# Four chained layers on one core: row statistics of three norms taken by ScalarE one stage earlier

## Chip, cores and metric

The kernel runs on one core of a Trainium2 chip, as one launch. The metric is the device time of a run in microseconds (us), lower is better; several runs are taken and their median counts. Engines are named PE (TensorE), DVE (VectorE), ACT (ScalarE), POOL (GpSimd) and SP (SyncE, which here only issues transfers).

## Reference, cut to what matters

A batch of 4 x 512 tokens with 256 channels passes through four layers, all in float32:

```python
def _layernorm(x, axis=-1, eps=1e-05):
    m = jnp.mean(x, axis=axis, keepdims=True)
    v = jnp.var(x, axis=axis, keepdims=True)
    return (x - m) / jnp.sqrt(v + eps)

x = L0_attn_x
xn = _layernorm(x); x = x + scan_attention(xn) + mlp(xn)                  # layer 0
xn = _layernorm(x); x = x + dilated_attention(xn) + moe_32_experts_top4(xn) # layer 1
xn = _layernorm(x); x = x + chunk_abc(xn) + mla_block_with_8_experts(xn)    # layer 2
xn = _layernorm(x); x = x + causal_attention(xn) + moe_8_experts_top2(xn)   # layer 3
```

The change concerns the second, third and fourth of these layer norms. The bodies of the layers are shortened to names here.

## The kernel before

The 2048 tokens are 16 tiles of 128 rows. `core.x` holds x in SBUF as [128, 16, 256]; `core.xn` holds the normalised rows, in rows of 260 columns whose last four, `core.marks`, are free until a routing writes its marks into them. The program is a sequence of blocks. In a block each engine has its own instruction stream, and at its end all five engines meet, so the next block starts when the last engine is done. The blocks that matter:

- `layer0_join` (j0): PE multiplies, ACT copies, POOL and DVE add, DVE takes statistics of another norm; then DVE alone writes `core.x` tile by tile (L807 the gain, L803 the sum, signalled by `added`).
- `slots_route` for layer 1 (p1) with `Normalise` n1: DVE takes the statistics (`part_stats`, L258 to L275) of tiles 0 to 7 and 8 to 15, POOL raises the variance to the power -0.5 (L304), DVE writes the normalised rows (L288), PE turns each tile (L319), ACT copies it into `xnT` (L338), and the routing follows: PE's logits, DVE's top choices and row numbers, then 64 indirect transfers by POOL (L2487), beside which the dilated attention runs.
- `slots_experts` (f1), the 32 experts. It ends with `add_pairs` (L2855), 64 additions of DVE into `core.x`, 8 for each group of two tiles.
- `NormaliseSplit` (n2): the same norm, but ACT copies each turned tile rounded (L403), DVE takes the rest (L389), and at the eighth tile ACT waits for the first six weight transfers and rounds the weights (L401).
- `layer2_abc`, `layer2_attention`, then `experts` (f2), eight dense experts in 32 steps of 512 tokens. `weigh` (L2421) adds each step's four tiles into `core.x` and raises `y_taken`. PE is saturated there until the last steps.
- `slots_route` for layer 3 (p3): PE first multiplies two weights (L3326, 16 matmuls), which ACT copies (L3332, L3335), ACT loads a table (L350), and then comes `Normalise` n3 as above with a small logits product behind each tile (L2686), and a second norm `own_norm` of the rows just written (r_...), whose statistics DVE still takes. Then `layer3_attention` (a3) and `slots_experts3` (f3).

What sets the order is the program text of each engine. Waits are on semaphores; `Steps` is a helper that makes an engine wait for its own last instruction before the next:

```python
    def __call__(self, instruction):
        instruction.then_inc(self.sem, 1)
        self.n += 1
        self.eng.wait_ge(self.sem, self.base + self.n)
```

Of the kernel before, what the change touches and what calls it, by code (L numbers as in the profile page):

```python
# [21 lines left out]
ALU = mybir.AluOpType  # L22
# [179 lines left out]

class Normalise:
# [8 lines left out]
    def __init__(self, st, core, src, tok_out, out_T, eps, rms=False, gain=None, shift=None, also_load=None, ring=4,  # L212
                 turned=None, parts=2, row=None, banks=None):
# [3 lines left out]
        self.raw = st.sb("raw", [P, TILES, 6])  # L217
        self.mean, self.var, self.rstd = (st.sb(n, [P, TILES]) for n in ("mean", "var", "rstd"))
# [58 lines left out]
    def tile_row(self, dve, t):  # L277
        if t % self.PER == 0:
            dve.wait_ge(self.rstd_ready, t // self.PER + 1)
            if not self.rms:  # L280
                dve.wait_ge(self.mean_ready, t // self.PER + 1)
        if self.tok_out is None and t >= self.ring:
            dve.wait_ge(self.rows_turned, t - self.ring + 1)
        if self.rms:
            dve.tensor_scalar(self.row_of(t), self.src[:, t, :], self.rstd[:, t:t + 1], None, ALU.mult
                              ).then_inc(self.rows_ready, 1)
        else:
            dve.tensor_scalar(self.row_of(t), self.src[:, t, :], self.mean[:, t:t + 1], self.rstd[:, t:t + 1],  # L288
                              ALU.subtract, ALU.mult).then_inc(self.rows_ready, 1)
# [17 lines left out]
    def gpsimd(self, pool):  # L307
        for part in range(self.parts):
            self.part_power(pool, part)
# [59 lines left out]
class NormaliseSplit(Normalise):  # L369
# [5 lines left out]
    def __init__(self, st, core, src, tok_out, dst, eps, w):  # L375
        Normalise.__init__(self, st, core, src, tok_out, None, eps, also_load=w.load_first)
        self.dst, self.w, self.hi_out = dst, w, st.sem("hi_out")

    def vector(self, dve):
        for part in range(self.parts):  # L380
            self.part_stats(dve, part)
# [337 lines left out]
def layer0_join(nc, st, core, w, gsT, gateT):  # L719
# [10 lines left out]
    names = "diag_ready sums_back ff_back rows_copied x_added y_ready stats dve_step var_ready rstd_ready gained added".split()  # L730
    s = {n: sem(n) for n in names}
    with nc.Block() as block:
        @block.scalar
        def _(act):
# [28 lines left out]
        def _(pool):  # L763
            for half in range(2):
                tiles = slice(half * HALF, (half + 1) * HALF)
                for t in range(half * HALF, (half + 1) * HALF):
# [5 lines left out]
                                   ).then_inc(s["rstd_ready"], 1)  # L772

# [1280 lines left out]
def experts(nc, st, core, spec, aT, router, also_load):  # L2054
# [136 lines left out]
    act_waited, pool_waited = sem("act_waited"), sem("pool_waited")  # L2191
    if not swiglu:
# [22 lines left out]
    with nc.Block() as block:  # L2215
# [79 lines left out]
        def _(act):  # L2295
# [30 lines left out]

            def body(i, first, last):
                for k in range(STEPS):
# [16 lines left out]
                    if piece_after(k) and not (last and k // PER == U - 1):  # L2345
                        split_weights(i, k, first)

            rounds(act, body)
            split_hidden(ROUNDS - 1, STEPS - 1)

        @block.gpsimd
        def _(pool):
# [17 lines left out]
            rounds(pool, body)  # L2370

# [488 lines left out]
def slots_experts(nc, st, core, r):  # L2860
# [11 lines left out]
    def wait_landed(eng, c, pieces):  # L2872
# [4 lines left out]
        else:  # L2877
# [16 lines left out]
             "y_ready y_copied rows_step rows_found cw_turned cw_copied bias_ready bias_added added").split()  # L2894
# [4 lines left out]
    with nc.Block() as block:  # L2899
# [96 lines left out]
        def _(act):  # L2996
# [32 lines left out]
            for i in range(NP + 3):  # L3029
# [6 lines left out]
                if i >= 3:  # L3036
                    copy_y(i - 3)

        @block.gpsimd
        def _(pool):  # L3040
            for k, limit in enumerate((spec.limit, spec.limit + 1.0)):
                pool.memset(limits[:, k, :], limit).then_inc(s["limits_ready"], 1)
            for i in range(NP):
                pool.wait_ge(s["rows_found"], 2 * i // CH + 1)
                pool.wait_ge(s["y_copied"], i + 1)
                for j in range(2):
                    b = 2 * i + j
                    pool.indirect_dma_start(r.ys[:, :], bass.IndirectOffsetOnAxis(ap=r.to_row[:, b:b + 1], axis=0),  # L3048
                                            yb[:, i % YR, j, :], None).then_inc(stored[i % YR], 16)

# [486 lines left out]
def build(nc, dram, out):  # L3537
    with ExitStack() as keep:
# [6 lines left out]
        core.xn, core.marks = core.rows[:, :, 0:D], core.rows[:, :, D:ROW]  # L3545
        core.consts = resident("consts", [P, C_END])
# [36 lines left out]
        if 2 in LAYERS:  # L3583
            release(nc, used)

            with ExitStack() as scope:
# [112 lines left out]
```

## Time and profile before

| | us |
|---|---|
| median of 3 runs | 2124.78 (2124.61 to 2125.85) |
| the profiled execution, its own time | 2104.8 |
| its span, first to last instruction | 2102.9 |
| PE busy | 1800.2 (86%) |
| DVE busy | 1394.7 (66%) |
| ACT busy | 740.2 (35%) |
| POOL busy | 578.4 (28%) |

The profiled execution is 20 us shorter than the median of the runs. The share of busy time is an average over some fifteen blocks with different limits, so the places at which blocks meet are read one by one. In the views, a line such as "118.68 0.48 DVE L803 ..." gives the start in us, the duration in us, the engine and the line; a number in brackets is the idle time of the engine before it and who ended it.

### The profile page before, as it was taken

What the parts mean: (1) busy time and instruction counts of PE and PEld (TensorE: products, weight loads), DVE (VectorE), ACT (ScalarE), POOL (GpSimd) and SP (SyncE); (2) the same over time, 40 slices, a digit from 0 to 9 for tenths busy, and PEclk for the clock granted to TensorE, in tenths of its full rate; (3) what the DMA queues carried; (4) which work ended last, traced back from release to release, by engine and by line L of the source; (5) the groups of instructions that cost most, each with busy time, mean ns of one, the idle gap of its engine ahead of it and who ended that gap; (6) DMA issues with size and microseconds to landing.
All of it is one profiled execution on the core that took longest, in us unless ns stands there. A gap on an engine that the chain in (4) does not pass through costs nothing. (4 is left out here: it accounts for less than half of the span.)

```text
span 2102.9 us, 37015 instructions
## 1 busy us (share of the span) xinstructions
PE 1800.2 (86%) x13832; PEld 1433.3 (68%) x13832; DVE 1394.7 (66%) x2980; ACT 740.2 (35%) x1733; POOL 578.4 (28%) x550
## 2 busy tenths in 40 slices
PE   5844189944999999999999997999988997989995
PEld 2432177833899999999899985455566875767773
DVE  5588255548787777777787775666656777644444
ACT  2424134422333343434333333145534323322221
POOL 1326735540121221212221112622232103511111
PEclk9976699975999999999999997989998996999998
DMA  9448244443000000000000100000001007111114
GB/s 324 142 132 269 88 136 146 149 150 111 1 1 24 24 2 24 1 24 1 24 1 24 34 1 1 0 1 2 2 1 53 29 1 251 62 43 48 49 49 140
DMA packets 103060, 134.86 MB, mean 64 GB/s; under 512 B 11628, under 2 KB 78984, under 8 KB 102376
## 3 DMA queue, kind: packets, MB, share of 16 engines
q1 hardware_dynamic: 91800, 102.01, 15.5%
q0 software_dynamic: 11088, 30.49, 4.0%
q8 instruction: 116, 1.90, 0.4%
q14 instruction: 56, 0.46, 0.1%
HBM read 81.92 MB, written 50.54 MB: 63 GB/s over the span
## 5 line engine op out<-in xcount | busy, mean ns | idle before, releaser
L1138 POOL TENSOR_TENSOR a_rstd<-a_msq,consts 128x8 f32<-128x8 f32 x32 | 52.4, 1636 | 556.2 <-DVE a_msq L1493 556.2
L110 PE MATMUL a_ring<-a_w_hi,l_xnT_hi 128*128 128x256 f32 x512 | 152.0, 297 | 0.0
L110 PE MATMUL a_ring<-a_w_hi,l_xnT_lo 128*128 128x256 f32 x512 | 144.6, 282 | 0.0
L110 PE MATMUL a_ring<-a_w_lo,l_xnT_hi 128*128 128x256 f32 x512 | 144.4, 282 | 0.0
L2487 POOL DMA_INDIRECT l_slots_in<-xn,f_row_of x96 | 105.2, 1096 | 82.0 <-DVE f_row_of L2815 37.0
L3048 POOL DMA_INDIRECT l_pairs_out<-f_yb,f_to_row x96 | 94.6, 985 | 97.6 <-ACT f_yb L3023 70.9
L1450 DVE RECIPROCAL a_rT<-a_rT 128x256 f32<-128x256 f32 x64 | 111.5, 1744 | 0.0
L1739 PE MATMUL b_ring<-b_keys,b_qm 32*128 32x128 f32 (+2 forms) x896 | 94.2, 347 | 14.9 <-DVE b_nm L1952 9.4
L1905 ACT ACTIVATE b_work<-b_ring 128x1024 f32<-128x1024 f32 (+1 forms) x96 | 81.1, 881 | 65.1 <-PE b_ring L1746 64.1
L2942 PE MATMUL f_pgu<-f_gate_up_w,f_xT 128*128 x384 | 95.0, 391 | 5.5 <-ACT f_xT L3003 5.4
L1739 PEld LDWEIGHTS b_ring<-b_keys,b_qm 32*128 32x128 f32 x896 | 67.1, 198 | 46.4 <-issue 23.4
L110 PEld LDWEIGHTS a_ring<-a_w_hi,l_xnT_hi 128*128 128x128 f32 x512 | 97.5, 190 | 0.2 <-issue 0.2
L110 PEld LDWEIGHTS a_ring<-a_w_lo,l_xnT_hi 128*128 128x128 f32 x512 | 97.6, 191 | 0.0
L110 PEld LDWEIGHTS a_ring<-a_w_hi,l_xnT_lo 128*128 128x128 f32 x512 | 97.4, 190 | 0.0
L319 PE MATMUL n_turned<-consts,xn 128*128 128x128 f32 x96 | 24.9, 397 | 81.6 <-DVE xn L288 81.6
L3156 POOL DMA_INDIRECT l_pairs_out<-l_aT,f_to_row x39 | 37.2, 955 | 199.2 <-DVEq L3296 192.5
L3073 DVE TENSOR_TENSOR f_gu<-f_pgu,f_bias 128x256 f32<-128x256 f32 x96 | 40.8, 425 | 74.5 <-issue 41.4
L1746 PE MATMUL b_ring<-b_qm,b_keys 32*128 32x384 f32 (+3 forms) x512 | 87.4, 463 | 0.0
L1871 POOL TENSOR_SCALAR_AFFINE_SELECT b_work<-b_work 128x256 f32<-128x256 f32 x128 | 50.5, 407 | 127.3 <-ACT b_work L1905 125.3
L110 PE MATMUL a_ring<-l_xnT_hi,a_w_hi 128*128 128x512 f32 x192 | 79.8, 416 | 3.7 <-PEq L416 3.7
L2942 PEld LDWEIGHTS f_pgu<-f_gate_up_w,f_xT 128*128 128x128 f32 x384 | 70.7, 194 | 17.7 <-issue 9.3
L1407 ACT ACTIVATE a_on<-a_pde 128x128 f32<-128x128 f32 x256 | 66.7, 292 | 44.0 <-PE a_pde L1296 44.0
(514 smaller groups left out, 5359.6 us busy)
## 6 DMA issues: line engine op xcount, KB each, us to landing
l_slots_in<-l_zeros SPq DMA_DIRECT2D x4, 3120.0 KB, 22.2
f_xb<-l_slots_in SPq DMA_DIRECT2D x11, 1040.0 KB, 5.7
f_gate_up_w<-l_pairs_out SPq DMA_DIRECT2D x16, 512.0 KB, 8.7
l_slots_in<-l_zeros SPq DMA_DIRECT2D x3, 1690.0 KB, 19.0
f_xb<-l_slots_in SPq DMA_DIRECT2D x39, 130.0 KB, 2.1
f_down_w<-L_ffn_w_down_dram SPq DMA_DIRECT2D x1, 4096.0 KB
f_gate_w<-L_ffn_w_dram SPq DMA_DIRECT2D x2, 2048.0 KB, 11.1
f_up_w<-L_ffn_w_dram SPq DMA_DIRECT2D x2, 2048.0 KB, 19.7
```

What stands on the lines that cost most here:

```text
L110: ins = pe.matmul(out, a, b, start=start and k == 0, stop=stop and k == 2, **kw)
L1138: pool.tensor_tensor(rstd[:], msq[:], core.consts[:, C_HALF:C_HALF + 8], ALU.pow).then_inc(s["rstd_ready"], 1)
L1407: act.activation(sq[:, h, c, :], pov[:, h, c, :], ACT.Square, accum_out=ms[:, i:i + 1]).then_inc(s["sq_ready"], 1)
L1450: dve.reciprocal(rT[:, k % 2, cols], rT[:, k % 2, cols]).then_inc(s["r_ready"], 1)
L1739: return pe.matmul(ps[:, i, at:at + k1 - k0], qm[strip(j), p, c, b * T + q * P:b * T + (q + 1) * P], keys[strip(j), p, c, b * T + k0:b * T ...
L1746: return pe.matmul(ps[:, i, at:at + T - kb * P], keys[strip(j), p, c, b * T + kb * P:b * T + (kb + 1) * P], qm[strip(j), p, c, b * T + kb ...
L1871: ins = pool.affine_select(x, x, [[0, 2], [1, P]], ALU.is_ge, 0.0, 0, -1)
L1905: act.activation(probs[:, g % 2, 2 * pair:2 * pair + 2, T_AT[k]:T_AT[k] + w], slot["t", g, pair, k][:, :, 0:w], ACT.Exp).then_inc(s["exp_r ...
L2487: pool.indirect_dma_start(self.xs[:, :], bass.IndirectOffsetOnAxis(ap=self.row_of[:, k, t:t + 1], axis=0), core.rows[:, t, :], None).then_ ...
L2942: ins = pe.matmul(pgu[:, i % 2, j * 2 * I:(j + 1) * 2 * I], xT[:, i % 2, (j * DC + c) * P:(j * DC + c + 1) * P], r.gate_up[:, bass.ds(e, 1 ...
L3048: pool.indirect_dma_start(r.ys[:, :], bass.IndirectOffsetOnAxis(ap=r.to_row[:, b:b + 1], axis=0), yb[:, i % YR, j, :], None).then_inc(stor ...
L3073: dve.tensor_tensor(gu[:, i % GR, j].rearrange("p k i -> p (k i)"), pgu[:, i % 2, j * 2 * I:(j + 1) * 2 * I], r.bias[:, bass.ds(e, 1), :, ...
```

## The change

In three blocks ACT takes over the row statistics of the norm that opens the next block. A new class `RowStats` keeps four numbers per row in `core.marks` (sum, minus a sixteenth of the mean, minus the mean, variance). For two tiles ACT does: a Copy of each tile into `core.xn` with a running sum, two small scalings of the sums, and a Square of each tile, again with a running sum. This happens in `layer0_join` behind DVE's additions, in `slots_experts` behind each group's additions, and in `experts` behind each of the last four `weigh`s; there the condition in `last_block` holds for none of the 16 steps in the loop, so that all four calls come after ACT's last `split_hidden`. POOL adds eps and takes the power for tiles 0 to 7 at the end of the old block and for tiles 8 to 15 at the start of the new one. In the new block DVE starts with the rows at once. The norm of the first block and `own_norm` keep their statistics on DVE.

```diff
+class RowStats:
+    def __init__(self, marks):
+        self.total, self.minus_16th, self.minus, self.var = (marks[:, :, k] for k in range(4))
+        self.rstd = self.minus_16th
+    def tiles(self, act, core, first, n, step, done):
+        cols = slice(first, first + n)
+        for t in range(first, first + n):
+            ins = act.activation(core.xn[:, t, :], core.x[:, t, :], ACT.Copy, accum_out=self.total[:, t:t + 1])
+        step(ins)
+        step(act.activation(self.minus_16th[:, cols], self.total[:, cols], ACT.Copy, scale=-1.0 / (16 * D)))
+        act.activation(self.minus[:, cols], self.total[:, cols], ACT.Copy, scale=-1.0 / D)
+        for t in range(first, first + n):
+            ins = act.activation(core.xn[:, t, :], core.x[:, t, :], ACT.Square, bias=self.minus_16th[:, t:t + 1],
+                                 scale=1.0 / 16, accum_out=self.var[:, t:t + 1])
+        ins.then_inc(done, 1)
+    def power(self, pool, core, half, eps, step, done):
+        n = TILES // 2
+        cols = slice(half * n, (half + 1) * n)
+        step(pool.tensor_scalar(self.var[:, cols], self.var[:, cols], eps, None, ALU.add))
+        pool.tensor_tensor(self.rstd[:, cols], self.var[:, cols], core.consts[:, C_HALF:C_HALF + n], ALU.pow
+                           ).then_inc(done, 1)
...
     def tile_row(self, dve, t):
+        if self.ahead is not None:
+            if t == TILES // 2:
+                dve.wait_ge(self.rstd_ready, 1)
+            dve.tensor_scalar(self.row_of(t), self.src[:, t, :], self.ahead.minus[:, t:t + 1],
+                              self.ahead.rstd[:, t:t + 1], ALU.add, ALU.mult).then_inc(self.rows_ready, 1)
+            return
...
     def vector(self, dve):
         for part in range(self.parts):
-            self.part_stats(dve, part)
+            if self.ahead is None:
+                self.part_stats(dve, part)
...
     def gpsimd(self, pool):
+        if self.ahead is not None:
+            self.ahead.power(pool, self.core, 1, self.eps, Steps(pool, self.shift_step), self.rstd_ready)
+            return
...
@@ layer0_join, scalar and gpsimd
+            step = Steps(act, s["act_step"])
+            for t in range(0, TILES, 2):
+                act.wait_ge(s["added"], t + 2)
+                core.row_stats.tiles(act, core, t, 2, step, s["squared"])
...
+            pool.wait_ge(s["squared"], HALF // 2)
+            core.row_stats.power(pool, core, 0, 1e-5, Steps(pool, s["pool_step"]), s["powered"])
@@ experts, scalar and gpsimd
+            def last_block(k):
+                behind = k - LAG - 2 - (U - 1) * PER
+                if behind >= 0 and behind % MC == MC - 1 and behind < PER:
+                    tb = behind // MC
+                    act.wait_ge(y_taken, 2 + E * BLOCKS - BLOCKS + tb + 1)
+                    for t in (4 * tb, 4 * tb + 2):
+                        core.row_stats.tiles(act, core, t, 2, row_step, squared)
...
             split_hidden(ROUNDS - 1, STEPS - 1)
+            for k in range(STEPS, STEPS + LAG + 3):
+                last_block(k)
...
+            pool.wait_ge(squared, TILES // 4)
+            core.row_stats.power(pool, core, 0, 1e-5, Steps(pool, power_step), powered)
@@ slots_experts, scalar and gpsimd
+            for g in range(GROUPS):
+                act.wait_ge(s["added"], 2 * K * (g + 1))
+                core.row_stats.tiles(act, core, 2 * g, 2, step, s["squared"])
...
@@ build
-                                      also_load=r1.load_first)
+                                      also_load=r1.load_first, ahead=core.row_stats)
...
-                                      also_load=r3.load)
+                                      also_load=r3.load, ahead=core.row_stats)
```

In this piece of ACT's stream, at the end of `layer0_join`, the join's copies (j_row) stood in front of the block's end and the next block's table load (before):

```order
L746 ACTIVATE j_row<-j_sums 128x256 x16
L732 UNCONDITIONAL_BRANCH
L2734 UNCONDITIONAL_BRANCH
L350 ACT_TABLE_LOAD
L338 ACTIVATE l_xnT<-n_turned 128x2x128 x11
```

And now (L215 the copies with a sum, L217 and L218 the small scalings, L220 the squares; the first of the eight pairs of tiles):

```order
L787 ACTIVATE j_row<-j_sums 128x256 x16
L215 ACTIVATE xn<-x 128x256 x2
L217 ACTIVATE xn<-xn 128x2
L218 ACTIVATE xn<-xn 128x2
L220 ACTIVATE xn<-x,xn 128x256 x2
```

Six instructions per pair of tiles moved in ahead of the block's end; no table load was added.

DVE's stream at the start of routing 1, before (the norm's statistics, tiles 0 to 7; the same eight rows follow once more for tiles 8 to 15, then the rows, L288):

```order
L258 BN_STATS n_raw<-x 128x6 x8
L268 TENSOR_TENSOR n_var<-n_raw 128x8
L269 TENSOR_TENSOR n_var<-n_var 128x8
L270 SCALAR_TENSOR_TENSOR n_var<-n_raw,n_var 128x8
L271 SCALAR_TENSOR_TENSOR n_var<-n_raw,n_var 128x8
L272 TENSOR_SCALAR n_var<-n_var 128x8
L274 TENSOR_TENSOR n_mean<-n_raw 128x8
L275 TENSOR_SCALAR n_mean<-n_mean 128x8
```

And now, from the end of the join (L850 its last additions) on:

```order
L850 SCALAR_TENSOR_TENSOR x<-xn,j_rstd,x 128x256 [waits j0_x_added,j0_rstd_ready,j0_gained] x2
L773 UNCONDITIONAL_BRANCH
L2821 UNCONDITIONAL_BRANCH [waits barrier_Pool_Activation_PE_DVE_SP_release]
L313 TENSOR_SCALAR xn<-x,xn 128x256 x8
L313 TENSOR_SCALAR xn<-x,xn 128x256 [waits n1_rstd_ready]
L313 TENSOR_SCALAR xn<-x,xn 128x256 x7
L2826 TENSOR_SCALAR f_bias<-consts 128x512
```

The rows open the block; only the ninth waits, for POOL's second power. The same happens at the starts of n2 and p3.

ACT's stream at the end of the dense experts, now (f_silu and f_hidden_hi are the last steps' work; one of the eight pairs of tiles):

```order
L2401 ACTIVATE f_silu<-f_pg 128x512 [waits f1_pool_step,f1_stored2]
L2363 ACTIVATE f_hidden_hi<-f_raw 128x512 [waits f1_stored2] x2
L215 ACTIVATE xn<-x 128x256 [waits f1_back_in3]
L215 ACTIVATE xn<-x 128x256
L217 ACTIVATE xn<-xn 128x2 [waits f2_stats_step]
L218 ACTIVATE xn<-xn 128x2 [waits f2_stats_step]
L220 ACTIVATE xn<-x,xn 128x256 x2
```

All of the new work stands behind the last hidden split; semaphore names there are those of earlier blocks whose semaphores are used again.

## Rows read from the trace of the kernel before

**Rows 1.** Spans of the cores, whole run.

```profile
core 0: 2102.9 us, clock 0.925
```

**Rows 2.** Timeline, 119 to 150 us (start, duration, engine, line, operation, out<-in, count, idle before).

```profile
119.47 0.48 DVE L803 SCALAR_TENSOR_TENSOR x<-xn,j_rstd,x 128x256 f32<-128x256 f32 x1
...
129.76 0.88 DVE L803 SCALAR_TENSOR_TENSOR x<-xn,j_rstd,x 128x256 f32<-128x256 f32 x2
...
130.92 1.28 ACT L350 ACT_TABLE_LOAD   x1 [16.08 <-PEq L732]
130.96 2.71 DVE L258 BATCH_NORM_STATS2 n_raw<-x 128x6 f32<-128x256 f32 x8 [0.32 <-PEq L732]
...
138.84 5.55 DVE L288 TENSOR_SCALAR xn<-x,n_mean,n_rstd 128x256 f32<-128x256 f32 x16
...
140.02 4.12 ACT L338 ACTIVATE l_xnT<-n_turned 128x256 f32<-128x256 f32 x10 [7.82 <-PE n_turned L319]
```

**Rows 3.** Timeline, end of sparse experts 1 and start of normalisation 2.

```profile
462.88 25.42 DVE L2855 SCALAR_TENSOR_TENSOR x<-f_gate_up_w,f_weight,x 128x256 f32<-128x256 f32 x64 [17.55 <-DMA f_gate_up_w<-l_pairs_out]
...
490.09 2.71 DVE L258 BATCH_NORM_STATS2 n_raw<-x 128x6 f32<-128x256 f32 x8 [1.78 <-PEq L121]
...
492.50 0.47 SPq L1001 DMA_DIRECT2D a_w_raw<-L_attn_Wo_dram  x1
...
497.97 1.37 DVE L288 TENSOR_SCALAR xn<-x,n_mean,n_rstd 128x256 f32<-128x256 f32 x4
...
503.11 2.11 ACT L401 ACTIVATE a_w_hi<-a_w_raw 128x2304 fp32r<-128x2304 f32 x1
```

**Rows 4.** DMA issues, 488 to 530 us (count, KB each, us to landing).

```profile
a_w_raw<-L_attn_Wo_dram SPq DMA_DIRECT2D x2, 256.0 KB, 4.8
```

**Rows 5.** Timeline of DVE, end of the dense experts.

```profile
1726.53 1.65 DVE L2421 SCALAR_TENSOR_TENSOR x<-f_py,f_cw,x 128x256 f32<-128x256 f32 x4
...
1732.22 1.66 DVE L2421 SCALAR_TENSOR_TENSOR x<-f_py,f_cw,x 128x256 f32<-128x256 f32 x4 [0.30 <-PE f_py L110]
```

**Rows 6.** Timeline of PE, start of routing 3.

```profile
1735.87 1.96 PE L3326 MATMUL p_place<-w_qkvT 128*128 128x256 f32 x8 [3.69 <-PEq L121]
```

**Rows 7.** Timeline, start and end of normalisation 3.

```profile
1739.60 0.60 ACT L3335 ACTIVATE w_o_w<-p_sums 128x512 f32<-128x512 f32 x1 [1.13 <-PE p_sums L3326]
...
1744.93 1.26 ACT L338 ACTIVATE l_xnT<-n_turned 128x256 f32<-128x256 f32 x3 [3.44 <-PE n_turned L319]
...
1761.05 0.41 ACT L338 ACTIVATE l_xnT<-n_turned 128x256 f32<-128x256 f32 x1 [0.77 <-PE n_turned L319]
```

**Rows 8.** Timeline of ACT, an accumulating pass in the linear attention.

```profile
618.62 0.28 ACT L1407 ACTIVATE a_on<-a_pde 128x128 f32<-128x128 f32 x1 [1.14 <-PE a_pde L1296]
618.79 0.19 ACT L1407 ACTIVATION_READ_ACCUMULATOR a_on<-a_pde 128x1 f32 x1
618.88 0.27 ACT L1407 ACTIVATE a_on<-a_pde 128x128 f32<-128x128 f32 x1
```

**Rows 9.** Timeline of ACT, two keys' copies from SBUF with a scale operand.

```profile
170.23 0.92 ACT L899 ACTIVATE a_keys<-l_xnT,consts 128x256 f32<-128x256 f32 x2
```

**Rows 10.** Groups of ACT by form (busy us, mean ns | idle before).

```profile
L403 ACT ACTIVATE l_xnT_hi<-n_turned 128x256 fp32r<-128x256 f32 x16 | 6.1, 405 | 51.0 <-PE n_turned L319 50.9
...
L610 ACT ACTIVATE m_decay_col<-m_cols 128x2 f32<-128x2 f32 x1 | 0.2, 203 | 0.0
```

**Rows 11.** Stretches of PE (length, PE busy, instructions, granted clock, DMA share, GB/s).

```profile
119.50:120.00 0.50, 0.00 (x0) 0.50 0.00 0
...
1739.00:1739.50 0.50, 0.50 (x3) 1.00 0.48 164
...
1749.50:1750.00 0.50, 0.50 (x4) 0.50 0.98 369
```

**Rows 12.** Timeline, the same product at the low and the full clock.

```profile
1780.71 5.88 PE L3391 MATMUL a_pt<-l_aT,w_qkvT 128*128 128x512 f32 x8 [2.33 <-PEq L2651]
...
1794.19 3.60 PE L3391 MATMUL a_pt<-l_aT,w_qkvT 128*128 128x512 f32 x8
```

More of the change, by code:

```diff
@@ L212, in __init__ @@
     def __init__(self, st, core, src, tok_out, out_T, eps, rms=False, gain=None, shift=None, also_load=None, ring=4,
-                 turned=None, parts=2, row=None, banks=None):
+                 turned=None, parts=2, row=None, banks=None, ahead=None):
+        self.ahead, self.shift_step = ahead, st.sem("shift_step")
         self.core, self.src, self.tok_out, self.out_T, self.eps, self.rms = core, src, tok_out, out_T, eps, rms
@@ L216, in __init__ @@
         self.PER = TILES // parts
-        self.raw = st.sb("raw", [P, TILES, 6])
-        self.mean, self.var, self.rstd = (st.sb(n, [P, TILES]) for n in ("mean", "var", "rstd"))
+        if ahead is None:
+            self.raw = st.sb("raw", [P, TILES, 6])
+            self.mean, self.var, self.rstd = (st.sb(n, [P, TILES]) for n in ("mean", "var", "rstd"))
         if tok_out is None and row is None:
@@ L375, in __init__ @@
     def __init__(self, st, core, src, tok_out, dst, eps, w):
-        Normalise.__init__(self, st, core, src, tok_out, None, eps, also_load=w.load_first)
+        Normalise.__init__(self, st, core, src, tok_out, None, eps, also_load=w.load_first, ahead=core.row_stats)
         self.dst, self.w, self.hi_out = dst, w, st.sem("hi_out")
     def vector(self, dve):
-        for part in range(self.parts):
-            self.part_stats(dve, part)
         for t in range(TILES + self.BEHIND):
@@ L729, in layer0_join @@
     sums, ff = st.ps("sums", [P, SLOTS, 512]), st.ps("ff", [P, SLOTS, 512])
-    names = "diag_ready sums_back ff_back rows_copied x_added y_ready stats dve_step var_ready rstd_ready gained added".split()
+    names = ("diag_ready sums_back ff_back rows_copied x_added y_ready stats dve_step var_ready rstd_ready gained "
+             "added act_step squared pool_step powered").split()
     s = {n: sem(n) for n in names}
@@ L2191, in experts @@
     act_waited, pool_waited = sem("act_waited"), sem("pool_waited")
+    stats_step, squared, power_step, powered = (sem(n) for n in ("stats_step", "squared", "power_step", "powered"))
     if not swiglu:
@@ L2325, in split_weights @@
                 act.activation(w.hi[:, u, cols], w_raw[:, u, cols], ACT.Copy).then_inc(w_hi, 1)
+            row_step = Steps(act, stats_step)
+            def last_block(k):
[5 more added lines that the diff above has]
+                        core.row_stats.tiles(act, core, t, 2, row_step, squared)
             def body(i, first, last):
@@ L2346, in body @@
                         split_weights(i, k, first)
+                    if last:
+                        last_block(k)
             rounds(act, body)
             split_hidden(ROUNDS - 1, STEPS - 1)
+            for k in range(STEPS, STEPS + LAG + 3):
+                last_block(k)
         @block.gpsimd
@@ L2893, in slots_experts @@
     names = ("x_turned x_copied gu_ready setup_step limits_ready biased clipped silu_ready h_ready h_turned h_copied "
-             "y_ready y_copied rows_step rows_found cw_turned cw_copied bias_ready bias_added added").split()
+             "y_ready y_copied rows_step rows_found cw_turned cw_copied bias_ready bias_added added "
+             "act_step squared pool_step powered").split()
     s = {n: sem(n) for n in names}
@@ L3037, in _ @@
                     copy_y(i - 3)
+            step = Steps(act, s["act_step"])
+            for g in range(GROUPS):
+                act.wait_ge(s["added"], 2 * K * (g + 1))
+                core.row_stats.tiles(act, core, 2 * g, 2, step, s["squared"])
         @block.gpsimd
@@ L3049, in _ @@
                                             yb[:, i % YR, j, :], None).then_inc(stored[i % YR], 16)
+            pool.wait_ge(s["squared"], GROUPS // 2)
+            core.row_stats.power(pool, core, 0, 1e-5, Steps(pool, s["pool_step"]), s["powered"])
         @block.vector
@@ L3545, in build @@
         core.xn, core.marks = core.rows[:, :, 0:D], core.rows[:, :, D:ROW]
+        core.row_stats = RowStats(core.marks)
         core.consts = resident("consts", [P, C_END])
```

## Prediction

> **What bounds the kernel now.** I read first the spans of the cores: one core, 2102.9 us, mean granted clock 0.925 [rows 1]. The busy shares (PE 86%, ACT 35%) say that ACT has room on the whole. They don't say whether it has room in the three places where it gets new work, so I go to the timeline at each of them.
>
> At the end of the join DVE alone works. Its second addition starts at 119.47 and ends at 119.95, its last ends at 130.64; the next block opens with ACT's table load at 130.92, DVE's statistics at 130.96, the rows at 138.84 and ACT's first copy of a turned tile at 140.02 [rows 2]. So 7.88 us of DVE (138.84 - 130.96) stand between the block's start and the rows, and PE and ACT wait for them. The same chain stands at n2: 490.09 to 497.97, again 7.88 us, after additions that end at 488.30 [rows 3]. At f2 the last additions are those of four steps: the first of the four starts at 1726.53 and ends at 1728.18, the last ends at 1733.88 [rows 5]; routing 3 opens at 1735.87 [rows 6]. There the rows are not the only thing ahead of the norm: PE multiplies weights for 3.7 us, and ACT copies the second product from 1739.60 to 1740.20 and loads a table (1.28 us long, as the one in [rows 2]), so it is free at 1741.5; its first copy of a turned tile starts at 1744.93 [rows 7].
>
> **What one pair of tiles costs ACT.** A Square or Copy with a running sum is two instructions on ACT: in the linear attention a 128-column pass starts at 618.62, its ACTIVATION_READ_ACCUMULATOR at 618.79 with 0.19 us, the next pass at 618.88 [rows 8], so 0.26 us each, 0.09 of it for the read. Each further column costs (2.11 - 0.405)/(2304 - 256) us = 0.83 ns [rows 3, 10], 0.107 us for the other 128. That makes 0.36 us for a tile from PSUM with no operand. From SBUF with a per-row scale the keys' copies come 0.41 us apart (0.92 for two, each 0.51) [rows 9], against 0.27 by [rows 8] without the read. I take 0.50 us for a Square (per-row bias, SBUF, read) and, between the two, 0.39 for a Copy. The chain of a pair: the second read starts 0.39 + 0.30 = 0.69 us in and ends at 0.89; after it ACT waits for itself, 0.05 us by estimate; the first small scaling lasts 0.20 [rows 10]; another 0.05; the second takes 0.10 of ACT's time; two Squares 1.00. **Sum 2.3 us per pair**, and the last one ends 2.4 us after its start. Bounds: 1.9 if all four passes cost 0.36 and the small steps 0.46, 3.0 if nothing overlaps at all. I take 2.3, since operands and memory are those of [rows 9].
>
> The Trainium skill (ScalarE: Activation LUTs, What ACT_TABLE_LOAD costs) gives 186 ns + 0.833 ns per element, 93 ns more for a per-row operand, 93 ns of overlap between neighbours, and no price for reading the accumulator. By that page alone a pair would take about 1.9 us and the whole sum come out 5.6 us lower, at about +1; the trace has the read as an instruction of its own, 0.09 us each time, and I go by the trace.
>
> **The sum, place by place.**
>
> 1. Join and routing 1. DVE finishes two tiles every 1.58 us, ACT needs 2.3, so ACT falls behind at once. It starts at 120.0 (second addition done), begins the eighth pair at 120.0 + 7 x 2.3 = 136.1 and ends at 138.5, where DVE ended at 130.64: the block closes **7.9 us later**. In routing 1 the rows start at once, **7.9 us earlier**; the table load hides, since it ends 1.3 us in and the first turned tile comes 1.2 us in. POOL's second power (the old ones lasted 1.63 to 1.88 us) is done some 2.4 us in by estimate, DVE wants it after eight rows, 2.8 us in: free. If that cover goes it is a few tenths. POOL's scatter hangs on the routing and moves with it. Net 0.0. The weight loads that SP issues at the block's start come 7.9 us nearer to the scatter's first transfers; I leave that at 0, bound +1.
>
> 2. Sparse experts 1 and n2. DVE adds a group of two tiles in 25.42/8 = 3.18 us [rows 3]; ACT keeps up. Only the last pair shows: **+2.4**. In n2 the rows gain 7.9, but ACT rounds the first weights at the eighth tile. Before, that came 13.1 us into the block (503.11); now it would come at 5.2. The sixth load was issued 2.46 us in (492.50) and lands 4.8 us later [rows 4], so at 7.3: ACT waits 2.1 us and the whole chain of tiles with it. Gain **-5.8**, bounds -7.9 (the load lands earlier) and -5. Net -3.4. Late next is this load.
>
> 3. Dense experts and routing 3. All four new calls stand behind ACT's last hidden split, so nothing in the loop is delayed. ACT starts at 1728.2 (first of the four steps added), begins the eighth pair at 1744.3 and ends at 1746.7, where DVE ended at 1733.88: **+12.8**. In routing 3 the rows are ready long before PE wants them, so only the wait of ACT from 1741.5 to 1744.93 can go, 3.4 us. But PE now stands still for 15 us ahead of the weight product. After such a pause the granted clock is at its lower level: in the join ACT waits from 114.8 on with PE done (16.08 us idle at 130.92 [rows 2]) and the clock is at 0.50 (1.2 GHz) at 119.5, while at 1739 it was still 1.00 (2.4 GHz) after 4 us without work [rows 11]. The same product of eight matmuls takes 5.88 us at first and 3.60 later [rows 12], so the 3.7 us of L3326 become about 5.8. That leaves 1.3 of the 3.4. Then the tiles start at the full clock, instead of at 0.50 from 1744.5 on; at 0.50 a tile takes (1761.05 - 1744.93)/15 = 1.07 us [rows 7]. For three or so tiles I grant 0.4 each, 1.3 together. Gain **-2.6**, bounds 0 and -7.9. Net +10.2.
>
> Beyond that nothing is changed in the first norm, `own_norm` or the later stages. DVE's 16 removed statistics and their small steps are counted in the 7.88. Layer 3's weights start 12.8 us later but are wanted only in the attention after it.
>
> Sum: 0.0 - 3.4 + 10.2 = **+6.8 us**; in terms of the pair's price p it moves by 14 us for each us of p. Against the profiled execution (2104.8, span 2102.9) that is 2111.6. The median of the runs, 2124.78, is 20 us above that execution; I put the same difference on it: **2131.6**.
>
> **The rivals.**
>
> - *Clock (not slower).* PE keeps 2.4 GHz through the sixteen tiles of n3, because it comes to them straight from the weight product. Place: routing 3 from its sixth us on. Price: some 12 further tiles at 0.4 us, -5 us, so the sum falls to +1.8, 2126.6. It decides as soon as half of those tiles run at the full clock. The Trainium skill (TensorE: Matmul & The Clock Gate, Part 1) says that what follows the first busy stretch runs at 2.4 GHz, which is this case. Against it: from 1744.5 on PE showed matmuls without a gap and stayed at 0.50 at 1749.5 [rows 11]; two transposes and four 8-column products per tile don't lift it.
> - *A cheap pair (not slower, or faster).* ACT's reads and small steps hide behind the passes and p is 1.75. -7.7 us, sum -0.9, 2123.9; below p = 1.5 the kernel is faster. For: ACT's instructions do overlap by 0.1. Against: the two waits for itself are in the text, and four passes alone need 1.6. With the clock as well it comes to about -6, 2119: faster.
> - *The change doesn't do what it says*: POOL's second power comes late and the ninth row waits in all three norms, because POOL needs a us for a 128x8 sum of eps. +1 each where rows bind (two places), 2133.6.
> - *Dear pair*: p = 2.7 from SBUF accesses of DVE and ACT side by side: +5.6, 2137.2.
>
> **How the numbers follow.** The forecast with its own spread 0.50, dear pair 0.10, late power 0.05, clock 0.15, cheap pair 0.12, both together or something else that gains 0.08. The range runs from the cheap pair less a little, 2122.5, to the dear pair, 2138. A measurement can tell about 0.2%, 4.2 us, from no change: above 2129.0 lie the dear and late cases and most of the forecast, 0.60; within, the clock, the cheap pair and the forecast's low edge, 0.32; faster 0.08.
>
> **What would show it.** At the join and at f2 the last instruction before the block's end is ACT's read after a Square, 7.9 and 12.8 us later than DVE's last addition was; at f1 2.4 us behind it. L217 should start 2.3 us after the last L217. Rows (L313) open each of the three blocks. In n2 ACT should idle before the rounding of the weights, released by a DMA. In routing 3 the weight product should run at 0.50 at first. The forecast is wrong if a pair takes under 1.9 us, or if the tiles of n3 come in under 0.8 us each.

## The result, and the profile after

| | before | after |
|---|---|---|
| median of 4 runs | 2125.32 us (2124.61 to 2126.22) | 2142.26 us (2140.05 to 2144.55) |
| ratio of the runs, 95% interval | | 1.0082, 1.0070 to 1.0094 |
| profiled execution (its span) | 2104.8 us (2102.9) | 2140.05 us (2138.5) |

The change costs 17 us. The forecast was +6.8 us, 2131.6, range 2122.5 to 2138.0. The direction was right, the size was not, and the result lies outside the range.

The spans of the cores, after; before it was [rows 1]:

```profile
core 0: 2138.5 us, clock 0.914
```

The two profiles stand 35.6 us apart, the runs only 17. A second profile of the kernel before (`before_again`, below) has a span of 2120.6: 17.7 of the 35.6 us belong to the first profile of before and not to the change. From here on after is read against that second profile wherever the two profiles of before differ.

**The join.** Timeline of ACT at its end, two pairs of tiles, and the first rows of routing 1 (columns as in [rows 2]):

```profile
134.07 0.21 ACT L217 ACTIVATE xn<-xn 128x2 f32<-128x2 f32 x1
...
135.41 0.40 ACT L215 ACTIVATE xn<-x 128x256 f32<-128x256 f32 x1
...
136.33 0.21 ACT L217 ACTIVATE xn<-xn 128x2 f32<-128x2 f32 x1
...
137.57 0.19 ACT L220 ACTIVATION_READ_ACCUMULATOR xn<-x,xn 128x1 f32 x1
138.03 1.28 ACT L392 ACT_TABLE_LOAD   x1 [0.27 <-PEq L773]
139.32 1.19 ACT L380 ACTIVATE l_xnT<-n_turned 128x256 f32<-128x256 f32 x3
142.12 1.26 ACT L380 ACTIVATE l_xnT<-n_turned 128x256 f32<-128x256 f32 x3 [1.61 <-PE n_turned L361]
```

L217 comes 2.26 us after the last L217 (136.33 - 134.07), where 2.3 was forecast. DVE's last addition ended at 130.26, ACT's last read at 137.76: 7.5 us. The rows start at once. Two pauses are new: ACT's 1.61 us above, and PE's under it. Timeline of DVE, then of PE:

```profile
138.06 5.55 DVE L313 TENSOR_SCALAR xn<-x,xn 128x256 f32<-128x256 f32 x16 [7.80 <-PEq L773]
```

```profile
138.53 1.54 PE L361 MATMUL n_turned<-consts,xn 128*128 128x128 f32 x6 [24.05 <-DVE xn L313]
141.42 3.22 PE L361 MATMUL n_turned<-consts,xn 128*128 128x128 f32 x14 [1.34 <-ACT l_xnT L380]
```

**The end of f1.** At a block's closing line each engine's queue has a record called DRAIN, and the next block opens after the last of them has ended. The record can start while the engine's last work still runs, so its end is what counts. Timeline of POOL there, then of DVE, then the records of the closing line, L2965 (duration in ns, start in us):

```profile
503.07 10.29 POOL L228 TENSOR_SCALAR xn<-xn 128x8 f32<-128x8 f32 x1 [22.24 <-ACT xn L220]
513.44 1.69 POOL L229 TENSOR_TENSOR xn<-xn,consts 128x8 f32<-128x8 f32 x1
524.88 0.26 POOL L228 TENSOR_SCALAR xn<-xn 128x8 f32<-128x8 f32 x1 [9.76 <-POOLq L121]
```

```profile
509.60 3.64 DVE L2920 SCALAR_TENSOR_TENSOR x<-f_gate_up_w,f_weight,x 128x256 f32<-128x256 f32 x9
524.89 1.38 DVE L313 TENSOR_SCALAR xn<-x,xn 128x256 f32<-128x256 f32 x4 [11.64 <-PEq L121]
```

```profile
L2965 DVEq DRAIN  x1: 797/797/797, 512.5 to 512.5; - x1
L2965 POOLq DRAIN  x1: 9651/9651/9651, 513.4 to 513.4; - x1
L2965 ACTq DRAIN  x1: 1211/1211/1211, 514.5 to 514.5; - x1
```

DVE is done at 513.24 and ACT at 515.65, 2.4 us later, as forecast. But the block closes at 523.05 (513.40 + 9.65), when POOL's DRAIN ends, 7.9 us after POOL's power did (513.44 + 1.69 = 515.13). The tail, from DVE's last addition to the end of the block, is 9.8 us. POOL's power comes that late because the instruction in front of it (L228, which adds eps to 128x8 values) lasts 10.29 us here, until DVE's last addition; at the start of n2 the same instruction takes 0.26 us. The first row of n2 comes 11.64 us after DVE's last addition; before it was 9.67 (488.30 to 497.97 [rows 3]). The norm gives back less than the tail costs.

In n2 ACT does wait for the weights ahead of rounding them (timeline of ACT):

```profile
531.74 2.12 ACT L441 ACTIVATE a_w_hi<-a_w_raw 128x2304 fp32r<-128x2304 f32 x1 [1.34 <-DMA a_w_raw<-L_attn_Wo_dram]
```

**f2 and routing 3.** Timeline of DVE, then of PE, over the seam:

```profile
1758.17 1.66 DVE L2486 SCALAR_TENSOR_TENSOR x<-f_py,f_cw,x 128x256 f32<-128x256 f32 x4 [0.30 <-PE f_py L110]
1774.35 5.26 DVE L313 TENSOR_SCALAR xn<-x,xn 128x256 f32<-128x256 f32 x16 [14.51 <-PEq L121]
```

```profile
1774.34 3.75 PE L3398 MATMUL p_place<-w_qkvT 128*128 128x256 f32 x8 [16.21 <-PEq L121]
1777.89 3.00 PE L3398 MATMUL p_sums<-w_o_w,w_qkvT 128*128 128x256 f32 x8
1780.72 0.82 PE L361 MATMUL n_turned<-consts,xn 128*128 128x128 f32 x6
...
1784.42 0.42 PE L361 MATMUL n_turned<-consts,xn 128*128 128x128 f32 x2
...
1789.37 0.67 PE L361 MATMUL n_turned<-consts,xn 128*128 128x128 f32 x2
```

From the last addition to the first product it takes 14.5 us (1759.83 to 1774.34), 12.5 more than before (1733.88 to 1735.87 [rows 5, 6]). The eight matmuls of [rows 6] take 3.75 us now, at a granted clock of 0.50 (1.2 GHz).

### The profile page after: what moved, and what is told of

The parts are those of the page before. It is cut to its first block and busy times, and to the rows that moved or that the text cites. A ratio compares the mean times of both kernels' runs of the same rounds, so it can differ in the third digit from the quotient of the medians.

```text
span 2138.5 us, 37165 instructions
## 1 busy us (share of the span) xinstructions
PE 1813.6 (85%) x13832; PEld 1438.2 (67%) x13832; DVE 1372.8 (64%) x2890; ACT 793.4 (37%) x1973; POOL 585.2 (27%) x556
## 5 line engine op out<-in xcount | busy, mean ns | idle before, releaser
L2552 POOL DMA_INDIRECT l_slots_in<-xn,f_row_of x96 | 98.2, 1023 | 104.3 <-DVE f_row_of L2880 42.6
L361 PE MATMUL n_turned<-consts,xn 128*128 128x128 f32 x96 | 24.6, 391 | 80.5 <-DVE xn L313 79.2
```

Source lines behind the costliest of these rows:

```text
L2552: pool.indirect_dma_start(self.xs[:, :], bass.IndirectOffsetOnAxis(ap=self.row_of[:, k, t:t + 1], axis=0), core.rows[:, t, :], None).then_ ...
```

## The experiments

Four jobs, each with its own runs of before beside it: the first four rows of the table, the next four, the next three and the last four. The kernel before takes 2122 to 2125 us in the first two, on two chips, and 2102 to 2103 in the last two, on a third, so differences are taken within a job.

| run | before beside it | median | difference | ratio, 95% |
|---|---|---|---|---|
| before_again | 2122.4 | 2122.0 | -0.4 | 0.9989 to 1.0008 |
| only_n1 | 2122.4 | 2124.7 | +2.3 | 1.0001 to 1.0020 |
| only_n2 | 2122.4 | 2126.0 | +3.6 | 1.0008 to 1.0029 |
| only_n3 | 2122.4 | 2133.5 | +11.1 | 1.0037 to 1.0072 |
| drain_alone | 2124.7 | 2133.4 | +8.7 | 1.0026 to 1.0054 |
| n2_late_power | 2124.7 | 2121.4 | -3.4 | 0.9973 to 0.9992 |
| half_n3 | 2124.7 | 2124.9 | +0.2 | 0.9988 to 1.0007 |
| halves_n1_n2late | 2124.7 | 2116.9 | -7.8 | 0.9953 to 0.9978 |
| all_late_power | 2102.1 | 2113.3 | +11.2 | 1.0041 to 1.0075 |
| bursts_of_four | 2102.1 | 2095.0 | -7.1 | 0.9957 to 0.9978 |
| bursts_of_four_tight | 2102.1 | 2095.5 | -6.6 | 0.9961 to 0.9981 |
| change_again | 2103.1 | 2121.1 | +18.0 | 1.0058 to 1.0114 |
| late_power_again | 2103.1 | 2114.4 | +11.3 | 1.0044 to 1.0079 |
| halves_again | 2103.1 | 2095.6 | -7.5 | 0.9950 to 0.9975 |
| bursts_again | 2103.1 | 2095.7 | -7.4 | 0.9954 to 0.9986 |

**1. A second profile of before.** No edit.

> The kernel before, unchanged, for a second profile of it. Its first profile shows a span of 2102.9 us, some 20 us below the 2124.6 to 2126.2 of its runs. In it linear attention 1 (layer 1's attention, beside the scattered rows) goes from 184 to 224 us without a stop, and the experts' stage f1 starts at 261.2. The changed kernel's profile has that attention stop and go from 184 to 278, and f1 starts at 280.3. Theory USUAL (the stop-and-go is how this stretch goes in most executions of either kernel, and the first profile of before was the exception): this profile has a span of 2123 to 2125 and f1 starts at 278 to 281. Theory CAUSED (the stop-and-go comes with the change): span near 2103, f1 at 261, and then the 20 us between profile and runs lie in some other stage.

USUAL holds: span 2120.6, f1's first load at 277.96. What ended ACT's waits beside the scatter (window 186 to 262 us), first in the first profile of before, then in the second (us in total, times, longest):

```profile
ACT a_sums L916 <- PE a_out L868: 7.9, 8, 1.7
ACT a_e L910 <- PE n_turned L859: 1.7, 4, 0.8
```

```profile
ACT a_e L910 <- remote: 27.9, 5, 8.9
ACT a_sums L916 <- remote: 23.5, 3, 13.4
```

"remote" stands where no instruction of the trace ends near the semaphore's update: PE's matmul has been over for 4 to 13 us when its update comes. All profiles of the first two jobs show this, none of the last two jobs: there routing 1 and its attention take 121 to 126 us, in the first two 141 to 148. It stands in before and after alike and goes with the chip or its state; since the last two jobs share a chip, the record can't say which of the two; it makes 16.4 us of the gap between the profiles (146.66 against 130.30 us for that block).

**2. One norm at a time.** `only_n1`, `only_n2`, `only_n3` each keep one of the three parts, e.g.

```diff
-            step = Steps(act, s["act_step"])
-            for g in range(GROUPS):
-                act.wait_ge(s["added"], 2 * K * (g + 1))
-                core.row_stats.tiles(act, core, 2 * g, 2, step, s["squared"])
...
-            pool.wait_ge(s["squared"], GROUPS // 2)
-            core.row_stats.power(pool, core, 0, 1e-5, Steps(pool, s["pool_step"]), s["powered"])
...
-        Normalise.__init__(self, st, core, src, tok_out, None, eps, also_load=w.load_first, ahead=core.row_stats)
+        Normalise.__init__(self, st, core, src, tok_out, None, eps, also_load=w.load_first)
```

> Only the norm ahead of routing 1 has its statistics in the join on ScalarE; the other two norms are as before. Prediction: 0.0 us beside before (2125), in a range of -3 to +3. The first comparison of profiles says the routing reaches its scatter 1.3 us later. Theory USUAL: 2125 to 2128, f1 starting 0 to 2 us later than in the second profile of before. Theory CAUSED (the later weight loads, which follow the block's start, make the scatter and the attention beside it stop and go): 2140 to 2145, f1 at 280.

> Only the norm ahead of the linear attention of layer 2 has its statistics in f1 on ScalarE. Prediction: 2.4 us of tail, 5.8 us of gain, so -3.4: 2121.6 from a median of 2125. Rival (the tail of f1 costs more than the norm gives back, or the stage behind is bound by its weights): 2125 to 2130. The last of f1's additions to the first row of n2 should be about 3.4 us shorter than in before.

> Only the norm ahead of routing 3 has its statistics in the dense experts' stage f2. Prediction: 12.8 us of tail behind f2's last addition, 2.6 us gained, so +10.2: 2135.2. Rival (clock: the gap lets TensorE's clock fall earlier than before, and layer 3's attention starts at half clock): +15 or more, 2140. Rival (the changed kernel's +8.9 us between f2's last addition and p3's attention holds alone): 2134. If all three changes add up, the three differences sum to the +17 us of the changed kernel.

2.3 + 3.6 + 11.1 = 17.0: the parts add up to the whole. CAUSED falls: n1 alone costs 2.3 us and not 15 to 20. n3 is as forecast. n2 is 7 us off with the wrong sign, n1 2.3 off. A block that isn't edited still differs by up to 3 us between profiles (f1 takes 228.9 us in `before_again`, 231.5 to 231.9 in `only_n1`, `only_n3` and `half_n3`), so I read the seams between blocks and not their lengths. In `only_n1` the block of the join is 7.5 us longer (42.04 against 34.57) and the scores of the routing come 5.7 us earlier in theirs (10.1 us after the block's start, 15.8 before). In `only_n2` f1 again closes 9.8 us behind the last addition, and POOL's L228 again lasts as long. Timeline of POOL in `only_n2`:

```profile
497.42 10.29 POOL L228 TENSOR_SCALAR xn<-xn 128x8 f32<-128x8 f32 x1 [22.32 <-ACT xn L220]
507.79 1.68 POOL L229 TENSOR_TENSOR xn<-xn,consts 128x8 f32<-128x8 f32 x1
```

**3. The DRAIN by itself.** The kernel before, with one small write put behind POOL's indirect transfers in f1:

```diff
+            pool.wait_ge(s["added"], 2 * K * GROUPS)
+            pool.memset(limits[:, 0, 0:1], spec.limit)
```

> The kernel before, with one small memset put behind everything else on POOL in f1, waiting for DVE's last addition; nothing else is changed. In the profile of only_n2 POOL's last power in f1 ends at 509.47, and POOL's DRAIN at the block's end lasts until 517.40, 7.9 us longer, though ACT's last read had ended at about 509.8. Theory DRAIN (in a block in which POOL has issued indirect DMAs, the DRAIN behind its last work lasts some 8 us whatever that work is; before, it lay under DVE's additions): +8 us, f1's block closes 8 us after DVE's last addition, 2130. Theory POWER (the long end belongs to the power or to the passes of ACT): no difference, 2122.

+8.7, for 8 expected. Timeline of POOL and DVE, then POOL's record of the closing line in `drain_alone`, then the same in `before_again`, then in the join of the changed kernel:

```profile
509.66 0.10 POOL L3109 MEMSET f_limits<- 128x1 f32 x1 [32.93 <-DVE x L2912]
...
519.49 1.74 DVE L290 BATCH_NORM_STATS2 n_raw<-x 128x6 f32<-128x256 f32 x5 [9.89 <-PEq L121]
```

```profile
L2957 POOLq DRAIN  x1: 8024/8024/8024, 509.6 to 509.6; - x1
```

```profile
L2899 POOLq DRAIN  x1: 12387/12387/12387, 469.7 to 469.7; - x1
```

```profile
L773 POOLq DRAIN  x1: 1784/1784/1784, 130.4 to 130.4; - x1
```

A memset of 0.10 us is followed by 7.9 us of DRAIN, although POOL had been idle for 32.93 us and its indirect transfers were long over. In `before_again` the DRAIN ends at 482.1, also 7.9 us after POOL's last work (its last transfer ends at 474.21), but 24 us before DVE's last addition, and costs nothing. In the join of the changed kernel, where POOL issues no indirect transfer, the power ended at 130.45 + 1.68 = 132.13 and the DRAIN at 132.2. So DRAIN holds, and POWER falls. This run shows what work behind the last addition costs. It doesn't test why the changed kernel's power came so late, which is the stretched L228.

**4. The same statistics, without work on POOL in f1.**

```diff
-            pool.wait_ge(s["squared"], GROUPS // 2)
-            core.row_stats.power(pool, core, 0, 1e-5, ...)
...
+        for part in range(self.parts):
+            if part * self.PER < self.n_ahead:
+                self.ahead.power(pool, self.core, part, self.eps, step, self.rstd_ready)
```

> As only_n2 (statistics of the linear attention's norm on ACT in f1), but both of POOL's powers stand in n2's block and POOL has nothing behind its indirect DMAs in f1. Theory DRAIN: the block of f1 closes 2.4 us after DVE's last addition instead of 9.8; in n2 the rows start 2.1 us into the block (a sum of 0.26 and a power of 1.68) and the wait of ACT for the weights (1.25 us in only_n2) is gone, so n2 gives back about 6: net -3.5 beside before, 2119, and 7 us less than only_n2. Theory POWER (ACT's passes themselves make the end long): the block still closes 9 to 10 us after the last addition, 2125 to 2128.

-3.4, for -3.5 expected here. Timeline of ACT, POOL and DVE:

```profile
512.62 0.19 ACT L220 ACTIVATION_READ_ACCUMULATOR xn<-x,xn 128x1 f32 x1
...
514.75 0.27 POOL L228 TENSOR_SCALAR xn<-xn 128x8 f32<-128x8 f32 x1 [36.80 <-POOLq L121]
...
515.10 1.68 POOL L229 TENSOR_TENSOR xn<-xn,consts 128x8 f32<-128x8 f32 x1
...
516.81 1.38 DVE L313 TENSOR_SCALAR xn<-x,xn 128x256 f32<-128x256 f32 x4 [6.41 <-POOL xn L229]
```

The block closes with ACT's last read, and the first row comes 6.4 us after the last addition instead of 11.6, though it now waits for a power. From the last addition to PE's first matmul behind the norm it takes 24.6 us in `before_again`, 27.7 in `only_n2` and 21.4 here, so the seam accounts for both medians: +3.1 beside +3.6, and -3.2 beside -3.4.

**5. Half of n3.**

```diff
-                if behind >= 0 and behind % MC == MC - 1 and behind < PER:
+                if behind >= 0 and behind % MC == MC - 1 and behind < PER // 2:
```

with DVE's `part_stats` for tiles 8 to 15 in routing 3.

> Only the norm ahead of routing 3 is changed, and ACT takes the statistics of its first eight tiles alone (four pairs) behind f2; DVE takes those of the other eight in routing 3, and both powers stand there. By the prediction's model (a pair every 2.26 us from the first of the four steps added, about 1.7 us after the last four additions begin): the block closes 3.5 us after DVE's last addition instead of 12.8; routing 3 gives back up to 3.4 us, less what a lower clock takes. Net 0 to +3.5, 2122 to 2126, against +11 with all eight pairs. Rival (the end of f2 is not set by the number of pairs): +8 or more.

+0.2, at the low edge of what was expected. The product starts 5.50 us after the last addition, 3.5 more than before, and four pairs fewer are 9.0 us less, 2.25 each (timeline of DVE, then of PE):

```profile
1751.70 1.66 DVE L2482 SCALAR_TENSOR_TENSOR x<-f_py,f_cw,x 128x256 f32<-128x256 f32 x4 [0.30 <-PE f_py L110]
```

```profile
1758.86 3.75 PE L3388 MATMUL p_place<-w_qkvT 128*128 128x256 f32 x8 [7.20 <-PEq L121]
```

PE had been idle for 7.20 us, and the product came at a granted clock of 0.50 just as after 16 us.

**6. A version that gains.** n1's statistics for its first eight tiles alone in the join (`range(0, HALF, 2)`), n2 as in 4, n3 as before.

> A version meant to gain: n1's statistics only for the first eight tiles in the join (four pairs end at 129.1 by the pair's 2.26 us, under DVE's additions, which end at 130.6), DVE takes those of the other eight in the routing, ahead of all rows, and POOL's powers stand in the routing; n2 as in n2_late_power; n3 as before. Join: 0. Routing 1: the rows start 4.0 us into the block instead of 7.9, so -3.9, or less if PE pauses as in only_n1 (there 1.3 us in its seventh matmul). f1 and n2: -3.5. Sum -7.4, 2115. Rival (what is gained ahead of the scatter is lost in the stop-and-go of the attention beside it): -3.5, 2119.

-7.8 here, for -7.4 expected, and -7.5 in `halves_again`: some 0.35% faster than before in each of two jobs. Four pairs end in the join at 128.61, DVE's last addition at 130.13, so the block is no longer. The scores of the routing come 11.7 us into it instead of 15.8. PE shows no pause in `halves_n1_n2late`; here its row, and under it that of `only_n1`, which has one:

```profile
134.84 4.18 PE L362 MATMUL n_turned<-consts,xn 128*128 128x128 f32 x20 [20.48 <-DVE xn L313]
```

```profile
139.16 1.54 PE L361 MATMUL n_turned<-consts,xn 128*128 128x128 f32 x6 [24.03 <-DVE xn L313]
142.04 3.22 PE L361 MATMUL n_turned<-consts,xn 128*128 128x128 f32 x14 [1.34 <-ACT l_xnT L380]
```

**7. The whole change without the DRAIN, and shorter bursts.** `all_late_power` moves both powers of all three norms into the norm's own block. The bursts are `halves_n1_n2late` with `SENT = 4` and a wait for mask n - 3 (tight: n - 2).

> The whole change (all sixteen statistics of the three norms on ACT), with one thing different: both of POOL's powers stand in the block of the norm, none in the stage ahead, so that POOL has nothing behind its indirect DMAs in f1. Theory DRAIN: f1's block closes 2.4 us after DVE's last addition, and the sum of the parts measured one by one holds: n1 +2.3 and 2 us more since the rows now wait for the first power, n2 -3.4, n3 +11.1 (there the power hides under the weight product): +12 at most and +10 if the later rows save routing 1 its pause, so 2135 to 2137 beside 2142 for the change, from a before of 2125. Rival (there is another cause that shows only with all three together): 2140 or more.

> As halves_n1_n2late, and the scatter beside attention 1 is sent in lots of four indirect DMAs instead of eight: lot n waits for mask n-3. In all later profiles PE's updates of its semaphores come 4 to 13 us late during the scatter, from some 6 us after POOL goes on until 2 us after POOL stops again; the attention takes from 184 to 277 us so, and 40 us where this does not happen (the first profile of before). Theory HELD BY THE STREAM (short lots with a stop behind each let PE's updates through before they pile up): the attention keeps step with the scatter, f1 starts at 255 to 265 instead of 274, total 2098 to 2108. Rival (the lateness is not tied to how long POOL sends without a stop, or each stop costs POOL what it gains PE): 2112 to 2125.

> As bursts_of_four, but lot n waits for mask n-2, so POOL is one tile of the attention less ahead and stops more often. HELD BY THE STREAM: as bursts_of_four or up to 5 us better, 2095 to 2108. Rival: POOL stops longer and the scatter itself ends later than the attention, 2115 to 2130.

This job ran where before takes 2102 us and nothing holds the attention up. So the bursts had nothing to cure: -7.1 and -6.6, the same as halves. In these profiles it is POOL that closes routing 1's block, as in the first profile of before (timeline of POOL, then its record of the closing line):

```profile
254.72 0.96 POOL L2487 DMA_INDIRECT l_slots_in<-xn,f_row_of  x1 [0.30 <-issue]
```

```profile
L2651 POOLq DRAIN  x1: 20462/20462/20462, 240.5 to 240.5; - x1
```

The other four engines are done there by 226.0; POOL's last transfer ends at 255.68 and its DRAIN at 260.96, 5.3 us later. So a DRAIN stood on the path in the kernel before already, wherever the attention doesn't stop. `all_late_power` had no changed kernel beside it, so four kernels were run once more together:

> The changed kernel itself, to stand on the same chip as the next run. +15 to +19 us beside before, as first measured, if the chip makes no difference; in its profile f1's block closes 9.8 us after DVE's last addition.

> The whole change with both powers in the block of the norm. DRAIN: 7.4 us less than change_again, +7 to +11 beside before. On a chip where the attention does not stop, routing 1 gave back 8.06 us of the join's 7.48 in the first profile of this kernel; if the same holds here the n1 part is 0 and what only_n1 lost (+2.3) came from PE's pause in its seventh matmul. If n1 costs 2 us here all the same, it is lost in the stretch of the attention.

> The same kernel as halves_n1_n2late, as the other side of the next comparison: -7 to -8 us beside before on any chip.

> The same kernel as bursts_of_four. On a chip on which before takes 2102 us it was equal to halves within a microsecond, as there was nothing to hold up. On a chip on which before takes over 2115 us, HELD BY THE STREAM says 8 to 18 us less than halves_again; the rival says the same as halves_again within 3 us. If before takes about 2102 us here too, the question stays open.

The change costs +18.0, and f1 closes 9.8 us after the last addition again; without POOL's work in f1 it costs +11.3: 6.7 us apart for 7.4 expected. The change costs the same, within the intervals, where before takes 2103 us as where it takes 2125, so the attention's stops show no part in it. `bursts_again` equals `halves_again`; before again took 2103, so whether short bursts would help where the attention stops is open. Late power's routing 1 starts its rows 2.5 us into the block, its PE has no pause, and its scores come 10.9 us in, against 9.9 to 10.6 with the pause.

## Why the prediction was wrong

- **A pair costs 2.3 us.** Right: 2.26, the last one ends 2.4 after its start. The Trainium skill's prices (ScalarE: Activation LUTs, What ACT_TABLE_LOAD costs), by which I had worked out 1.9, are too low here; a read again takes 0.1 us of its own (491.43 to 491.53 in f1).
- **Point 1, join and routing 1, net 0.** The join closed 7.5 us later (7.9 forecast), and the rows opened the block where they had come 7.9 us into it, as forecast. But only 5.7 us of that reached the scores. Of the missing 2.2 us, 1.5 is PE's pause: its seventh turned matmul comes 2.9 us after its first, where `before_again` needs 1.3. I had counted the cover for the table load and for POOL, not that PE itself might not be ready so early in a block. Net +1.8 by the two profiles, +2.3 by the medians.
- **Point 2, f1 and n2, net -3.4.** This is the step that failed: "Only the last pair shows: +2.4". ACT's pair did end 2.4 us behind, but the change had put two instructions of POOL behind the 96 indirect transfers of f1, and the forecast has no term for POOL there. The tail was 9.8. Two things make it: POOL's DRAIN, which ends 7.9 us after POOL's last work, and POOL's L228 of 10.29 us, which held that work back until DVE's last addition. With 0.26 us for L228 POOL would have been done at 505.1 and its DRAIN, by the same 7.9, at 513.0, before ACT; that is an estimate from these rows, and no run tests the stretch of L228 by itself. In n2 ACT waited 1.34 us for the load (2.1 forecast). The pair of blocks cost +3.6, 7.0 more than forecast. With POOL's work taken out of f1 it gives -3.4, the very number of the forecast, but not by its terms: there the rows wait 2.1 us for a power, and ACT doesn't wait for the load. That agreement is partly luck.
- **Point 3, f2 and n3, net +10.2.** The tail was right: 12.5 (12.8 forecast), and the whole part costs +11.1. Routing 3 gave back 0.7 us in `only_n3`, `change_again` and both late kernels, and 3.6 in the first profile of after and in `half_n3`, where five tiles came 0.64 us apart before the clock fell and the rest 1.17. The forecast's 2.6 lies between, so its size is partly luck. One premise was off: that the weight product takes 3.7 us in before. That is so in the first profile alone. It takes 5.4 in `before_again`, 6.4 in `bursts_again` after only 3.74 us without work, and 6.5 to 6.7 with the long tail (5.8 forecast; the ratio quoted for it gives 6.0). Most of that price was paid in before already.
- **Sum.** 6.8 forecast, 17.0 by the three parts (16.9 and 18.0 by the whole change). Of the 10.2 missing, 7.0 are n2, 2.3 n1, 0.9 n3.
- **The rivals.** The cheap and the dear pair were rivals on a term that came out as forecast. The clock rival needed half of some twelve further tiles at the full clock; in two profiles five had it, in four none. "Late power" was right to suspect POOL and its sum of eps, and looked at the wrong block: it asked when the ninth row gets its power, at +1 us each, and not how long that sum lasts beside DVE's additions in f1 and what stands between POOL's last instruction and the end of its block.
- **The median.** The 20 us between profile and runs was put on the sum unchanged; that was right: 17.7 of them lie in the first profile and not in the kernel.

## What to carry to other kernels

Before an engine gets a last piece of work in a block, look at what its end costs there: in the records of the block's closing line, a DRAIN that lies under other engines' work is free only until something is put behind it. Ask too how long a short instruction of POOL can last beside a row of DVE's: here 10.29 us for 0.26. Work that is moved onto a free engine pays only while that engine keeps step: of two tiles per 1.58 us ACT could take half (2.26 us a pair), and the half gained where the whole cost. Where a profile lies apart from the runs, take it again before reading differences stage by stage.

## What the runs showed of the hardware

- **POOL's DRAIN.** In f1, where POOL has issued 96 indirect transfers, the DRAIN ends 7.9 us after POOL's last work: 515.13 to 523.05 behind a power, 509.76 to 517.66 behind a memset, 474.21 to 482.12 behind the last transfer itself. In the join, without such transfers, 0.07 us. The other blocks of `before_again` line up by the number of such transfers in them: 1.7 us behind the last work with 4 of them, 2.8 with 28, 3.2 with 39, 5.3 with 64. From 39 to 96 that is 0.083 us for each. No run changed the number alone.
- **A small instruction of POOL beside DVE's additions.** L228 adds a constant to 128x8 values. It takes 0.26 to 0.39 us at the norm's start, beside rows (L313, one tensor from SBUF), but 10.29 us beside L2920 and 1.54 in the join, and each time it ends 0.1 us after DVE's last addition (513.36 and 513.24, 130.37 and 130.26; in `only_n2` 507.71 and 507.58). The Trainium skill (GPSIMD Engine Reference, 1. Specifications) says that POOL's access to SBUF is shared with VectorE and contends with instructions that have two SBUF inputs; the trace agrees, and here the wait was not one addition of 0.48 us long but the whole row of them.
- **PE at a block's start.** In the three profiles in which n1's rows start with the block (after, `only_n1`, `change_again`), PE's seventh matmul comes 3.6 to 3.8 us after the block before has closed, its semaphores long raised. In the other profiles of that block PE's first matmul comes 3.0 us or more after the close, and there is no such pause. In n2 of the changed kernel the first comes 2.3 us and the seventh 3.6 us after the close, without a pause. No record shows the cause.
- **Updates that come late.** In the first two jobs PE's semaphore updates came 4 to 13 us late beside POOL's stream of indirect transfers, and the same program was 20 us slower than in the last two. In after's profile a backlog cleared 2 to 3 us behind a stop of POOL (at 200.7 and 226.9, POOL's last transfers ending at 197.5 and 224.6), but others came while it was sending. The cause is open.
